# Two first products in full fp32, a shorter warm-up from a constant, and one load moved to another queue

## The chip, the core and the metric

The kernel runs on one core of a Trainium2 chip. The metric is device time in microseconds of one execution, lower is better; the time of a version is the median of its runs. A profile is one more execution, taken with the hardware profiler.

## What is computed

x is 2 x 512 x 512, so 1024 tokens of 512 features. Two blocks follow each other, each with a residual and a layer norm (all in fp32):

```python
# block 1
approx_up = x @ up_w.T ; gate_pre = x @ gate_w.T            # 512 -> 128 each
delta = gate_pre - local_point
approx_out = approx_up @ local_approx_output.T
for idx in range(6):                                         # Taylor-like terms of |delta|
    m = idx + 1
    dterm = exp(log|delta| * m - discount_factor[idx]) (* sign of delta if m is odd)
    tmp = dterm * approx_up (* (|delta| <= 2.5) if m > 4)
    approx_out += tmp @ fuse_weight[:, :, idx].T
ffn_out = silu(x @ ffn_gate_w.T) * (x @ ffn_up_w.T) @ ffn_down_w.T   # width 1248
x = layernorm(x + approx_out + ffn_out)
# block 2: weights first quantised to NF4 by blocks of 64 and dequantised, width 1376
x = layernorm(x + silu(x @ dq(w1).T) * (x @ dq(w2).T) @ dq(w3).T)
```

## The kernel before, in words

x is loaded transposed, with features on the partitions: four chunks `c` of 128 features by 1024 tokens, and each chunk has two halves `a` of 512 tokens (`HALF`). Below, x0a is chunk 0, first half, x0b its second half, x1a chunk 1, first half, and so on. They land in `xT_raw`, which is the start of the tile `h`; the profile calls them `h<-xT`.

TensorE's products are not plain fp32. Each operand is split into two fp32r numbers: ScalarE rounds it (`x_hi`, `w_hi`, in a helper at line 567), VectorE or GpSimd takes the remainder (`x_lo`, `w_lo`; lines 1032, 1037 and 1041 at the start), and TensorE adds up hi*hi, hi*lo and lo*hi, three matmuls of up to 512 columns. Everything but the two first stages below goes through the helper `product`, lines 1257 to 1259.

The first stage is the pair `up_w`, `gate_w`, together `w_pre`: for each of the four chunks, both `kind`s (0 and 1) and both halves, into the PSUM banks `2 * kind + half`. w_pre is loaded in three parts, 128 KB for chunk 0, 128 KB for chunk 1, 256 KB for the rest. TensorE takes chunk 0 by lines 1371 to 1382, six products for each half: for both kinds hi*hi (line 1376), w_lo*x_hi (1379), w_hi*x_lo (1382). Chunks 1 to 3 follow through `product`, and then the pairs of the gate and up weights (`w_in`), the output stage, and block 2. All of it is one fixed order on each engine, written out by hand, and engines wait for each other by counting semaphores.

Ahead of chunk 0 TensorE runs a warm-up: `WARM` fp32 products of 256 columns with zeros (line 1367) into an unused bank. The zeros are written by GpSimd into the tile `level` (line 1222), and TensorE waits for them.

The loads are issued by SyncE (`block.sync`) in this order: w_pre's first part, w_pre's second part (line 522), x1a, x1b (526), w_pre's rest (529), chunk 2 and chunk 3 (530), then w_in, the NF4 weights and so on (508, 511). ScalarE issues x0a and x0b (line 701) ahead of its first computation. The weights pass through five slots of the tile `raw` (`RAW_SLOTS`); load job `j` uses slot `j % 5`, and job 5 waits (`wait_split`) until job 0, which is w_pre, has been split.

Of the kernel before, what the change touches and what calls it, by code (L numbers as in the profile page):

```python
# [22 lines left out]
F32 = mybir.dt.float32  # L23
# [6 lines left out]
P = 128  # L30
TOK = 1024
D = 512
DC = D // P
HALF = 512
# [12 lines left out]
EPS = 1e-5  # L47
NR = 4
NL = 3
WARM = 5  # L50
BLOCK = 64
TINY = 1.1754943508222875e-38

# [71 lines left out]
def unit_width(u):  # L125
    if u < C2:
        return 2 * DC * min(P, F2 - u * P)
    return D * min(2, C2 - 2 * (u - C2))
# [55 lines left out]
RAW_SLOTS = 5  # L184
# [54 lines left out]
def rows(f, width):  # L239
    return min(P, width - f * P)  # L240


def job_rows(job):
    kind, f = job
    return P if kind == "fuse" else rows(f, F1) if kind == "out" else rows(f, F2)


def build(nc, xT, xN, w_pre, w_fuse, w_in, w_out, consts, w12, w3, w3_end, ident_in, out):
    with ExitStack() as ctx:  # L249
        def sb(name, shape, dt=F32):  # L250
            return ctx.enter_context(nc.sbuf_tensor(name, shape, dt))

        def sem(name):
            return ctx.enter_context(nc.semaphore(name))

        x_hi, x_lo = sb("x_hi", [P, DC, TOK], F32R), sb("x_lo", [P, DC, TOK], F32R)
# [6 lines left out]
        level = sb("level", [P, NL, UW])  # L263
# [8 lines left out]
        PS = ctx.enter_context(nc.psum_tensor("PS", [P, 8, 512], F32))  # L272

        xT_raw = h[:, 0:DC * TOK].rearrange("p (c t) -> p c t", c=DC)
# [21 lines left out]
        def w_raw(j):  # L296
            return raw[:, (j % RAW_SLOTS) * 1024:(j % RAW_SLOTS) * 1024 + 1024]

        def in_slot(w, i, n):
            return w[:, i % 2, 0:n]  # L300
# [14 lines left out]
        def job_shape(j):  # L315
            kind, f = JOBS[j]
            if kind == "pre":
                return P, 2 * DC * P
            if kind == "in":
                return P, 2 * DC * rows(f, F1)  # L320
            return job_rows(f), D
# [6 lines left out]

        s_line0 = sem("s_line0")
        s_ones = sem("s_ones")  # L330
        s_zero, s_warm = sem("s_zero"), sem("s_warm")
        s_pre_raw, s_pre_hi, s_pre_lo = [sem(f"s_pre_raw{c}") for c in range(2)], sem("s_pre_hi"), sem("s_pre_lo")
        s_point, s_ident = sem("s_point"), sem("s_ident")
        s_x = [sem(f"s_x{c}") for c in range(DC)]
        s_xb = [sem(f"s_x{c}b") for c in range(2)]
# [6 lines left out]
        s_xh, s_xl = sem("s_xh"), sem("s_xl")  # L342
        s_whi, s_wlo0, s_wlo = sem("s_whi"), sem("s_wlo0"), sem("s_wlo")
        s_wlo_in, s_wlo_v = sem("s_wlo_in"), sem("s_wlo_v")
        s_whi4, s_wlo4 = sem("s_whi4"), sem("s_wlo4")
        s_lhi, s_llo_t, s_llo_h = sem("s_lhi"), sem("s_llo_t"), sem("s_llo_h")
        s_pre, s_up, s_delta = sem("s_pre"), sem("s_up"), sem("s_delta")
        s_t, s_keep = sem("s_t"), sem("s_keep")
        s_pair, s_silu, s_h = sem("s_pair"), sem("s_silu"), sem("s_h")
# [21 lines left out]
        def wait_split(eng, j):  # L371

            if j < 2:
                eng.wait_ge(s_wlo0, j + 1)
            elif JOBS[j][0] == "in":
                eng.wait_ge(s_wlo_in, j - 1)
            elif j in VECTOR_LOW:
                eng.wait_ge(s_wlo_v, VECTOR_LOW.index(j) + 1)
            else:
                eng.wait_ge(s_wlo, j - C1 - sum(1 for x in VECTOR_LOW if x < j))  # L380
# [114 lines left out]
        @block.sync  # L495
        def _(sp):
            def load_job(j):
                kind, f = JOBS[j]
                if j >= RAW_SLOTS:
                    wait_split(sp, j - RAW_SLOTS)  # L500
                p, n = job_shape(j)
                if kind == "in":
                    src = w_in[:, f * 1024:f * 1024 + n]
                elif f[0] == "fuse":
                    src = w_fuse[f[1]]
                else:
                    src = w_out[f[1] * P:f[1] * P + p, :]
                sp.dma_start(w_raw(j)[0:p, 0:n], src).then_inc(s_raw[j % RAW_SLOTS], 16)

            def load_unit(u):  # L510
                sp.dma_start(unit_read(u), w12[:, u * UW:u * UW + unit_width(u)]).then_inc(s_q[u], 16)

            def load_residual(a):

                sp.wait_ge(s_llo_t, (G + 1) * (a + 1))
                sp.dma_start(R[:, TILES * a:TILES * (a + 1), :],
                             xN[:, TILES * a:TILES * (a + 1), :]).then_inc(s_R[a], 16)

            for c in range(DC):
                if c < 2:  # L520
                    part = slice(c * PRE0, (c + 1) * PRE0)
                    sp.dma_start(w_raw(0)[:, part], w_pre[:, part]).then_inc(s_pre_raw[c], 16)  # L522

                    for a in range(2 if c else 0):
                        ts = slice(a * HALF, (a + 1) * HALF)
                        sp.dma_start(xT_raw[:, c, ts], xT[:, c, ts]).then_inc((s_x, s_xb)[a][c], 16)
                    continue
                if c == 2:
                    sp.dma_start(w_raw(0)[:, 2 * PRE0:1024], w_pre[:, 2 * PRE0:1024]).then_inc(s_raw[0], 16)
                sp.dma_start(xT_raw[:, c, :], xT[:, c, :]).then_inc(s_x[c], 16)  # L530
            load_job(1)
            load_unit(0)
            sp.dma_start(term_consts[:], consts).then_inc(s_point, 16)
            load_unit(1)
            load_job(2)
            load_unit(2)
            for j in range(3, RAW_SLOTS):
                load_job(j)
            sp.dma_start(ident[:], ident_in).then_inc(s_ident, 16)
            for u in range(3, C2):  # L540
                load_unit(u)
            for j in range(RAW_SLOTS, len(JOBS)):
                if j == JOB[1, AGAIN[0]]:
                    load_residual(0)
                load_job(j)
            load_residual(1)
            for k in range(W3_UNITS):
                u = C2 + k
                if u < UNITS - 1:

                    wait_split(sp, max(j for j in range(len(JOBS)) if j % RAW_SLOTS == k))
                else:
                    sp.wait_ge(s_turn, 1)
                sp.dma_start(unit_read(u), (w3[:, k * UW:(k + 1) * UW] if u < UNITS - 1 else w3_end)).then_inc(s_w3[k], 16)

            for t in [t for t in range(TT) if t != TT - 2]:
                if t < TT - 1:
                    sp.wait_ge(s_norm, TT + t + 1)
                else:
                    sp.wait_ge(s_norm_last, 1)  # L560
                sp.dma_start(out[t * P:(t + 1) * P, :], R[:, t, :]).then_inc(s_out, 16)
            sp.wait_ge(s_out, 16 * TT)

        @block.scalar
        def _(act):
# [130 lines left out]
                copy(w_slot(2, ("w3", c), p)[0].rearrange("p (i b) -> p i b", i=SQ),  # L696
                     PS[0:p, w3_bank(c), :].rearrange("p (b i) -> p i b", i=SQ)).then_inc(s_whi4, 1)

            for a in range(2):
                ts = slice(a * HALF, (a + 1) * HALF)  # L700
                nc.scalar.dma_start(xT_raw[:, 0, ts], xT[:, 0, ts]).then_inc((s_x, s_xb)[a][0], 16)
            for c in range(DC):
                for a in range(2):
                    if c < 2 and a == 0:
# [6 lines left out]
                    ts = slice(a * HALF, (a + 1) * HALF)  # L711
# [60 lines left out]
            for n in range(PASS_START[2], len(SEQ)):  # L772
                if n + L_AHEAD < len(SEQ):
                    split_l(n + L_AHEAD)
                c = n - PASS_START[2]
# [390 lines left out]
        def _(pool):  # L1166
            g = nc.gpsimd
# [50 lines left out]
                pool.wait_ge(s_up2, k + 1)  # L1218
                g.tensor_tensor(dst, dst, up2[0:dst.shape[0], k % 2, :], ALU.mult).then_inc(s_h2, 1)  # L1219


            g.memset(level[:, 0, 0:P + 2 * P], 0.0).then_inc(s_zero, 1)
            for i in range(2 * C1):
                if i % 2 == 0 and i // 2 + 1 < C1:
                    lo_raw(JOB["in", i // 2 + 1])
# [27 lines left out]
        def _(pe):  # L1253
            t_ = nc.tensor
# [107 lines left out]
                last.then_inc(s_xtr, 1)  # L1362


            pe.wait_ge(s_zero, 1)
            for i in range(WARM):
                last = t_.matmul(PS[:, 7, 0:2 * P], level[:, 0, 0:P], level[:, 0, P:3 * P], start=True, stop=True)
            last.then_inc(s_warm, 1)
            wh0, wl0 = (in_slot(w, 0, 1024).rearrange("p (c g m) -> p g c m", g=2, c=DC) for w in (w_hi, w_lo))

            pe.wait_ge(s_pre_hi, 1)
            for half in range(2):
                xs = slice(half * HALF, (half + 1) * HALF)
                pe.wait_ge(s_xh, half + 1)
                for kind in (1, 0):
                    t_.matmul(PS[:, 2 * kind + half, :], wh0[:, kind, 0, :], x_hi[:, 0, xs], start=True, stop=False)
                pe.wait_ge(s_pre_lo, 1)
                for kind in (1, 0):
                    t_.matmul(PS[:, 2 * kind + half, :], wl0[:, kind, 0, :], x_hi[:, 0, xs], start=False, stop=False)
                pe.wait_ge(s_xl, half + 1)  # L1380
                for kind in (1, 0):
                    t_.matmul(PS[:, 2 * kind + half, :], wh0[:, kind, 0, :], x_lo[:, 0, xs], start=False, stop=False)
            for c in range(1, DC):
                if c == 1:
                    pe.wait_ge(s_pre_hi, 2)
# [4 lines left out]
                for kind, half in ((1, 0), (0, 0), (1, 1), (0, 1)) if c < DC - 1 else ((1, 0), (1, 1), (0, 0), (0, 1)):  # L1390
                    pe.wait_ge(s_xh, 2 * c + half + 1)
                    pe.wait_ge(s_xl, 2 * c + half + 1)
                    xs = slice(half * HALF, (half + 1) * HALF)
                    last = product(PS[:, 2 * kind + half, :], wh0[:, kind, c, :], wl0[:, kind, c, :],
                                   x_hi[:, c, xs], x_lo[:, c, xs], False, c == DC - 1)
# [21 lines left out]
            for n in range(PASS_START[2], PASS_START[3] - TAILS[2]):  # L1417
                c = n - PASS_START[2]
# [66 lines left out]
```

## Time and profile before

| | us |
|---|---|
| median of 3 runs | 411.65 (411.63 to 411.87) |
| the profiled execution | 412.71 |
| its span, first to last instruction | 410.8 |
| TensorE busy in it | 401.8 (98%) |
| VectorE, ScalarE, GpSimd busy | 325.1, 267.4, 290.1 |
| mean granted TensorE clock | 0.997 of full |

Times inside the profile count from the start of the span. `SPq` and `ACTq` are the issues of DMAs by SyncE and ScalarE, `PE` is TensorE's matmuls, `PEld` its weight loads. Matmul records overlap: one of 512 columns is drawn 0.39 us long while the next starts 0.23 us after it, so the distance between starts is what one costs.

### The profile page before, as it was taken

The page shows a single profiled execution, that of the slowest core. Times are in us where ns is not written, and L with a number is a line of the kernel's source. Part 1 is how long each engine was busy: PE and PEld are TensorE (multiplying, and loading weights), DVE is VectorE, ACT ScalarE, POOL GpSimd, SP SyncE. Part 2 cuts the span into 40 slices and gives each one's busy share as a digit, 9 for nine tenths or more (in the row PEclk, how much of TensorE's full clock was granted, in tenths as well). Part 3 has the DMA queues.
Part 4 walks back from the last instruction along what each step waited for, and adds up shares of the span by engine and source line. Part 5 has one row for each costly group of instructions (what it writes and reads, how often), then busy time and mean ns, then how long its engine had stood idle before and what let it go on. Part 6 is the DMA issues. An engine that isn't in the chain of part 4 may idle for free.

```text
span 410.8 us, 5355 instructions
## 1 busy us (share of the span) xinstructions
PE 401.8 (98%) x1770; PEld 327.9 (80%) x1770; DVE 325.1 (79%) x383; ACT 267.4 (65%) x372; POOL 290.1 (71%) x228
## 2 busy tenths in 40 slices
PE   7999999999999999999999999999999999999993
PEld 5888888888877888888888888888888877888872
DVE  3629989779888986999998799987779989935035
ACT  5575666677676847466956658888769777732613
POOL 0077998877978489936993366799999998954430
PEclk9999999999999999999999999999999999999998
DMA  7994101100204362103043000000000000000202
GB/s 258 409 408 146 53 14 51 28 26 0 53 3 123 89 224 69 27 0 104 1 131 146 0 2 1 2 0 0 2 2 0 2 0 0 2 0 2 102 0 102
DMA packets 10042, 26.48 MB, mean 64 GB/s; under 512 B 1248, under 2 KB 1632, under 8 KB 9760
## 3 DMA queue, kind: packets, MB, share of 16 engines
q1 hardware_dynamic: 9584, 25.37, 18.2%
q10 hardware_dynamic: 432, 0.79, 0.7%
q8 instruction: 14, 0.23, 0.2%
q14 instruction: 12, 0.10, 0.1%
HBM read 24.06 MB, written 2.10 MB: 64 GB/s over the span
## 4 chain that ended last, share of the span: by engine, by line
PE 95%; DMA 2%; DVE 1%; ACT 0%; issue 0%; POOLq 0%; SPq 0%; DVEq 0%; ACTq 0%
PE PS L1257 32%; PE PS L1258 31%; PE PS L1259 31%; DMA h<-xT 2%; PE PS L1361 1%; POOLq L249 0%; SPq L522 0%; ACT R L567 0%; DVE stats L933 0%; DVE R L928 0%; DVE x_lo L1041 0%; ACT x_hi L567 0%; ACT std L784 0%; DVE mv L959 0%; DVE std L972 0%
## 5 line engine op out<-in xcount | busy, mean ns | idle before, releaser
L1182 POOL TENSOR_SCALAR level<-side 128x1024 f32<-128x1024 int8 (+2 forms) x119 | 129.7, 1090 | 27.1 <-ACT side L567 13.0
L855 DVE TENSOR_TENSOR PS<-PS,level 128x1024 f32<-128x1024 f32 (+2 forms) x102 | 120.1, 1178 | 23.1 <-POOL level L1182 19.1
L1257 PE MATMUL PS<-x_hi,w_hi 128*128 128x512 f32 (+1 forms) x348 | 135.8, 390 | 0.9 <-DVE x_lo L1041 0.9
L1259 PE MATMUL PS<-x_hi,w_lo 128*128 128x512 f32 (+1 forms) x348 | 135.6, 390 | 0.0
L1258 PE MATMUL PS<-x_lo,w_hi 128*128 128x512 f32 (+1 forms) x348 | 135.5, 389 | 0.0
L567 ACT ACTIVATE side<-Q 128x1024 int8<-128x1024 f32 (+2 forms) x84 | 80.1, 997 | 17.2 <-DVE PS L851 15.2
L1257 PEld LDWEIGHTS PS<-x_hi,w_hi 128*128 128x128 f32 (+1 forms) x348 | 64.5, 185 | 16.1 <-issue 1.7
L1212 POOL TENSOR_TENSOR l_lo<-h,l_hi 128x512 fp32r<-128x512 f32 (+1 forms) x42 | 57.6, 1379 | 27.3 <-ACT l_hi L567 26.4
L1259 PEld LDWEIGHTS PS<-x_hi,w_lo 128*128 128x128 f32 (+1 forms) x348 | 64.5, 185 | 14.5
L1258 PEld LDWEIGHTS PS<-x_lo,w_hi 128*128 128x128 f32 (+1 forms) x348 | 64.5, 185 | 14.4
L1257 PE MATMUL PS<-x_hi,l_hi 128*128 128x512 f32 x144 | 56.1, 390 | 0.0
L1258 PE MATMUL PS<-x_lo,l_hi 128*128 128x512 f32 x144 | 56.1, 389 | 0.0
L1259 PE MATMUL PS<-x_hi,l_lo 128*128 128x512 f32 x144 | 56.0, 389 | 0.0
L650 ACT ACTIVATE h<-PS 128x512 f32<-128x512 f32 (+1 forms) x42 | 25.0, 594 | 34.3 <-PE PS L1259 34.0
L1201 POOL TENSOR_TENSOR w_lo<-raw,w_hi 128x1024 fp32r<-128x1024 f32 (+2 forms) x15 | 30.3, 2019 | 22.1 <-ACT w_hi L567 21.6
L1219 POOL TENSOR_TENSOR h<-h,Q 128x512 f32<-128x512 f32 (+1 forms) x22 | 30.3, 1376 | 18.2 <-ACT Q L567 15.9
L567 ACT ACTIVATE l_hi<-h 128x512 fp32r<-128x512 f32 (+1 forms) x42 | 25.9, 626 | 25.2 <-PE PS L1259 25.1
L567 ACT ACTIVATE side<-raw 128x1024 int8<-128x1024 f32 x35 | 35.1, 1058 | 6.1 <-DVE PS L851 6.1
L1257 PEld LDWEIGHTS PS<-x_hi,l_hi 128*128 128x128 f32 x144 | 27.0, 188 | 6.0 <-issue 0.4
L1257 PE MATMUL PS<-w_hi,l_hi 128*128 128x512 f32 (+1 forms) x80 | 31.5, 394 | 0.2 <-POOL l_lo L1212 0.2
L1259 PEld LDWEIGHTS PS<-x_hi,l_lo 128*128 128x128 f32 x144 | 27.0, 188 | 5.6
L1258 PEld LDWEIGHTS PS<-x_lo,l_hi 128*128 128x128 f32 x144 | 27.0, 188 | 5.6
(100 smaller groups left out, 510.6 us busy)
## 6 DMA issues: line engine op xcount, KB each, us to landing
Q<-w SPq DMA_DIRECT2D x10, 512.0 KB, 13.8
raw<-w_in SPq DMA_DIRECT2D x9, 512.0 KB, 12.3
raw<-w_out SPq DMA_DIRECT2D x14, 256.0 KB, 2.6
raw<-w SPq DMA_DIRECT2D x5, 512.0 KB, 3.8
R<-xN SPq DMA_DIRECT2D x2, 1024.0 KB, 5.4
raw<-w_fuse SPq DMA_DIRECT2D x7, 256.0 KB, 2.6
out<-R SPq DMA_DIRECT2D x7, 256.0 KB, 2.0
h<-xT SPq DMA_DIRECT2D x2, 512.0 KB, 8.1
```

The lines of the kernel that those rows point to most:

```text
L567: return nc.scalar.activation(dst, src, ACT.Copy, **kw)
L650: nc.scalar.activation(dst, PS[0:dst.shape[0], bank, :], ACT.Silu).then_inc(s_silu, 1)
L855: v.tensor_tensor(total, total, level_of(s), ALU.add).then_inc(s_add, 1)
L1182: g.tensor_scalar(level_of(s), side_of(s), LIMITS[k][1], LIMITS[k][0], ALU.min, ALU.max).then_inc(s_level, 1)
L1201: g.tensor_tensor(lo, w_raw(j)[0:p, 0:n], hi.bitcast(F32), ALU.subtract).then_inc(s_wlo_in if JOBS[j][0] == "in" else s_wlo, 1)
L1212: g.tensor_tensor(lo, view, hi.bitcast(F32), ALU.subtract).then_inc(s_llo_h, 1)
L1219: g.tensor_tensor(dst, dst, up2[0:dst.shape[0], k % 2, :], ALU.mult).then_inc(s_h2, 1)
L1257: t_.matmul(dst, a_hi, b_hi, start=start, stop=False)
L1258: t_.matmul(dst, a_hi, b_lo, start=False, stop=False)
L1259: return t_.matmul(dst, a_lo, b_hi, start=False, stop=stop)
L1361: last = t_.transpose(PS[:, XT_BANK + t % 2, c * P:(c + 1) * P], R[:, t, c * P:(c + 1) * P], ident[:])
```

## The change

TensorE's warm-up has four products in place of five and reads its zeros from the constant that the framework keeps (a 128 x 1 constant, repeated along the row), so that GpSimd's memset and the wait for it go. The first half of chunk 0 is computed by two fp32 products, one for each kind, straight from `raw` and `xT_raw`, in place of six split ones; the second half stays as it was, but waits for the counts that stood for half 1. x0a's load moves from ScalarE's queue to SyncE's, behind w_pre's first part; x0b stays on ScalarE's and is its only one. SyncE waits, ahead of job 5, which overwrites slot 0 of `raw`, until both fp32 products are done (`s_first`). ScalarE and VectorE still split x0a and w_pre, in the same order.

```diff
-WARM = 5
+WARM = 4
@@ load_job (SyncE)
                 if j >= RAW_SLOTS:
                     wait_split(sp, j - RAW_SLOTS)
+                if j == RAW_SLOTS:
+
+                    sp.wait_ge(s_first, 2)
@@ SyncE's first loads
                     sp.dma_start(w_raw(0)[:, part], w_pre[:, part]).then_inc(s_pre_raw[c], 16)
 
-                    for a in range(2 if c else 0):
+                    for a in range(2 if c else 1):
                         ts = slice(a * HALF, (a + 1) * HALF)
                         sp.dma_start(xT_raw[:, c, ts], xT[:, c, ts]).then_inc((s_x, s_xb)[a][c], 16)
@@ ScalarE
-            for a in range(2):
-                ts = slice(a * HALF, (a + 1) * HALF)
-                nc.scalar.dma_start(xT_raw[:, 0, ts], xT[:, 0, ts]).then_inc((s_x, s_xb)[a][0], 16)
+            nc.scalar.dma_start(xT_raw[:, 0, HALF:TOK], xT[:, 0, HALF:TOK]).then_inc(s_xb[0], 16)
@@ GpSimd
-            g.memset(level[:, 0, 0:P + 2 * P], 0.0).then_inc(s_zero, 1)
@@ TensorE
-            pe.wait_ge(s_zero, 1)
+            zeros = nc.const_aps.tensor(0.0, (P, 2 * P), F32)
             for i in range(WARM):
-                last = t_.matmul(PS[:, 7, 0:2 * P], level[:, 0, 0:P], level[:, 0, P:3 * P], start=True, stop=True)
+                last = t_.matmul(PS[:, 7, 0:2 * P], zeros[:, 0:P], zeros, start=True, stop=True)
             last.then_inc(s_warm, 1)
+            w_first = w_raw(0).rearrange("p (c g m) -> p g c m", g=2, c=DC)
+            pe.wait_ge(s_pre_raw[0], 16)
+            pe.wait_ge(s_x[0], 16)
+            for kind in (1, 0):
+                t_.matmul(PS[:, 2 * kind, :], w_first[:, kind, 0, :], xT_raw[:, 0, 0:HALF], start=True, stop=False).then_inc(s_first, 1)
             pe.wait_ge(s_pre_hi, 1)
-            for half in range(2):
-                xs = slice(half * HALF, (half + 1) * HALF)
-                pe.wait_ge(s_xh, half + 1)
...
+            pe.wait_ge(s_xh, 2)
+            for kind in (1, 0):
+                t_.matmul(PS[:, 2 * kind + 1, :], wh0[:, kind, 0, :], x_hi[:, 0, HALF:TOK], start=True, stop=False)
+            pe.wait_ge(s_pre_lo, 1)
+            for kind in (1, 0):
+                t_.matmul(PS[:, 2 * kind + 1, :], wl0[:, kind, 0, :], x_hi[:, 0, HALF:TOK], start=False, stop=False)
+            pe.wait_ge(s_xl, 2)
+            for kind in (1, 0):
+                t_.matmul(PS[:, 2 * kind + 1, :], wh0[:, kind, 0, :], x_lo[:, 0, HALF:TOK], start=False, stop=False)
```

## Rows read from the trace of the kernel before

**Rows 1.** The page: busy time by engine, and the chain that ended last by engine.

```profile
PE 401.8 (98%) x1770; PEld 327.9 (80%) x1770; DVE 325.1 (79%) x383; ACT 267.4 (65%) x372; POOL 290.1 (71%) x228
...
PE 95%; DMA 2%; DVE 1%; ACT 0%; issue 0%; POOLq 0%; SPq 0%; DVEq 0%; ACTq 0%
```

**Rows 2.** The chain that ended last, 0 to 12 us: start us, us, what.

```profile
1.64 6.56 DMA h<-xT
...
8.22 0.64 ACT x_hi L567
...
8.89 0.70 DVE x_lo L1041
...
9.72 0.47 PE PS L1257
```

**Rows 3.** The timeline of TensorE: start us, us, instruction, count, idle time before it.

```profile
5.83 0.70 PE L1376 MATMUL PS<-x_hi,w_hi 128*128 128x512 f32 x2
...
8.22 0.61 PE L1382 MATMUL PS<-x_lo,w_hi 128*128 128x512 f32 x2
...
11.85 0.39 PE L1257 MATMUL PS<-x_hi,w_hi 128*128 128x512 f32 x1
12.08 0.39 PE L1258 MATMUL PS<-x_lo,w_hi 128*128 128x512 f32 x1
12.31 0.39 PE L1259 MATMUL PS<-x_hi,w_lo 128*128 128x512 f32 x1
12.53 0.39 PE L1257 MATMUL PS<-x_hi,w_hi 128*128 128x512 f32 x1
```

**Rows 4.** The timeline, all engines: the start of the programs, and GpSimd's next work.

```profile
0.24 0.10 POOL L1478 MEMSET const-float32-0.0<- 128x1 f32 x1 [0.24 <-issue]
...
0.73 0.42 POOL L1222 MEMSET level<- 128x384 f32 x1 [0.29 <-POOLq L1478]
...
0.81 0.06 DVE L1022 MEMSET line<- 128x1 f32 x1 [0.81 <-PEq L1478]
...
1.20 4.56 PE L1367 MATMUL PS<-level 128*128 128x256 f32 x10 [1.20 <-POOL level L1222]
...
20.22 2.39 POOL L1201 TENSOR_TENSOR w_lo<-raw,w_hi 128x1024 fp32r<-128x1024 f32 x1 [19.07 <-ACT w_hi L567]
```

**Rows 5.** Timelines of warm-up records, cut so that their starts show; the transposes' chain row.

```profile
4.35 1.06 PE L1367 MATMUL PS<-level 128*128 128x256 f32 x2
...
4.78 0.99 PE L1367 MATMUL PS<-level 128*128 128x256 f32 x2
...
5.20 0.56 PE L1367 MATMUL PS<-level 128*128 128x256 f32 x1
...
195.41 0.87 PE PS L1361 x8
```

**Rows 6.** The timeline of ScalarE and VectorE: the splits of the first operands.

```profile
4.22 0.42 ACT L567 ACTIVATE w_hi<-raw 128x256 fp32r<-128x256 f32 x1 [1.28 <-DMA raw<-w_pre]
...
5.06 0.63 ACT L567 ACTIVATE x_hi<-h 128x512 fp32r<-128x512 f32 x1 [0.42 <-DMA h<-xT]
...
6.11 0.63 ACT L567 ACTIVATE x_hi<-h 128x512 fp32r<-128x512 f32 x1 [0.42 <-DMA h<-xT]
...
10.81 0.63 ACT L567 ACTIVATE x_hi<-h 128x512 fp32r<-128x512 f32 x1 [0.63 <-DMA h<-xT]
...
11.47 0.69 DVE L1041 TENSOR_TENSOR x_lo<-h,x_hi 128x512 fp32r<-128x512 f32 x1 [0.56 <-ACT x_hi L567]
```

**Rows 7.** The timeline of the DMA issues: SyncE's first ones and its first after a wait.

```profile
0.74 0.85 SPq L522 DMA_DIRECT2D raw<-w_pre  x2
1.64 0.90 SPq L526 DMA_DIRECT2D h<-xT  x2
...
3.06 1.01 SPq L530 DMA_DIRECT2D h<-xT  x2
...
18.02 2.32 SPq L508 DMA_DIRECT2D raw<-w_in  x2
```

**Rows 8.** Stretches of 1 us: busy by engine, clock, DMA share, GB/s.

```profile
2.00:3.00 1.00, 1.00 (x3) 0.80 (x3) 0.00 (x0) 0.94 (x1) 0.00 (x0) 1.00 0.92 281
3.00:4.00 1.00, 1.00 (x4) 0.75 (x3) 0.00 (x0) 0.00 (x0) 0.00 (x0) 1.00 1.00 203
...
7.00:8.00 1.00, 1.00 (x6) 0.79 (x6) 0.80 (x2) 0.05 (x1) 0.00 (x0) 1.00 1.05 391
```

More of the change, by code:

```diff
@@ L330, in build @@
         s_ones = sem("s_ones")
-        s_zero, s_warm = sem("s_zero"), sem("s_warm")
+        s_warm = sem("s_warm")
         s_pre_raw, s_pre_hi, s_pre_lo = [sem(f"s_pre_raw{c}") for c in range(2)], sem("s_pre_hi"), sem("s_pre_lo")
@@ L346, in build @@
         s_lhi, s_llo_t, s_llo_h = sem("s_lhi"), sem("s_llo_t"), sem("s_llo_h")
+        s_first = sem("s_first")
         s_pre, s_up, s_delta = sem("s_pre"), sem("s_up"), sem("s_delta")
@@ L1362, in transpose_x @@
                 last.then_inc(s_xtr, 1)
-            pe.wait_ge(s_zero, 1)
+            zeros = nc.const_aps.tensor(0.0, (P, 2 * P), F32)
             for i in range(WARM):
-                last = t_.matmul(PS[:, 7, 0:2 * P], level[:, 0, 0:P], level[:, 0, P:3 * P], start=True, stop=True)
+                last = t_.matmul(PS[:, 7, 0:2 * P], zeros[:, 0:P], zeros, start=True, stop=True)
             last.then_inc(s_warm, 1)
             wh0, wl0 = (in_slot(w, 0, 1024).rearrange("p (c g m) -> p g c m", g=2, c=DC) for w in (w_hi, w_lo))
-            pe.wait_ge(s_pre_hi, 1)
-            for half in range(2):
-                xs = slice(half * HALF, (half + 1) * HALF)
-                pe.wait_ge(s_xh, half + 1)
[L1375 to L1382, printed above, removed]
+            w_first = w_raw(0).rearrange("p (c g m) -> p g c m", g=2, c=DC)
[3 more added lines that the diff above has]
+                t_.matmul(PS[:, 2 * kind, :], w_first[:, kind, 0, :], xT_raw[:, 0, 0:HALF], start=True, stop=False).then_inc(s_first, 1)
+            pe.wait_ge(s_pre_hi, 1)
+            pe.wait_ge(s_xh, 2)
[7 more added lines that the diff above has]
+                t_.matmul(PS[:, 2 * kind + 1, :], wh0[:, kind, 0, :], x_lo[:, 0, HALF:TOK], start=False, stop=False)
             for c in range(1, DC):
```

## The prediction

> **What bounds the kernel now.** I read the page first, then the chain that ended last, then the first 13 us engine by engine, since every line of the change acts there. The page gives TensorE 401.8 of 410.8 us and the chain puts 95% on it, 2% on one transfer [rows 1]: the kernel is one long row of matmuls, and time can only be gained or lost where TensorE waits. The chain of the first 10 us shows the one early wait: the fourth DMA of the kernel (x's chunk 1, first half, "x1a" below) is issued at 1.64, lands 6.56 us later at 8.20, ScalarE rounds it (0.64), VectorE makes the remainder (0.70), and TensorE goes on at 9.72 [rows 2]. From there its products start 0.23 us apart up to 12.53, where chunk 2 begins [rows 3]. Before that wait TensorE had 12 products of chunk 0, the first at 5.83, the last pair from 8.22 [rows 3]; at 0.23 each they are issued out by 5.83 + 12 x 0.233 = 8.63. So it stands still for 9.72 - 8.63 = 1.1 us, and only for x1a. That is the fact on which all else hangs: whatever is done to chunk 0 before 9.72 is hidden as long as it is done by then, and nothing in it makes 9.72 earlier.
>
> **The warm-up.** It is five fp32 products of 256 columns, ten records, from 1.20 after a 0.42 us memset at 0.73 [rows 4]. The records start 0.427 us apart (4.35, 4.78, 5.20) [rows 5]. Each must be two passes of 256 columns, 512 column steps in 0.427 us, which is the 1.2 GHz level; from 5.83 a product of 512 columns takes 0.23 us, the 2.4 GHz level. The two passes are read from the transposes, whose records of 128 columns take 0.109 us, 256 steps at 2.4 GHz [rows 5]. So the granted clock rose between 5.2 and 6, after some 4.4 us of unbroken work; the clock column of the stretches says 1.00 from 2 us on already [rows 8], and there I go by the distance of the records. With the constant there is no memset to wait for. The constants are written by 0.24 and the other engines start their programs at 0.74 to 0.81 [rows 4], so I put TensorE's start at 0.8. One product less is 2 x 0.427 = 0.85 us less: the warm-up ends at 0.8 + 4.56 - 0.85 = 4.5 in place of 5.76. Cost and gain by themselves: nothing, as it lies before the wait. The memset off GpSimd is worth nothing either, since that engine next works at 20.22 [rows 4].
>
> **When the first product can start.** Now it needs w_pre's first part and x0a as loaded, and neither ScalarE's nor VectorE's pass. The first part of w_pre is ready at 4.22, x0a at 5.06, x0b at 6.11 [rows 6]. x0a came alone in ScalarE's queue with 512 KB moved in both queues; by the time of x0b, 768 KB were moved. With x0a second in SyncE's queue and x0b first in ScalarE's, x0a has up to 128 + 256 + 256 = 640 KB to share with. Halfway between 5.06 and 6.11 is 5.5, bounds these two. So the first product starts at about 5.6, 0.2 us before 5.83: what is saved on the roundings is mostly lost on the later x0a.
>
> **The fp32 pair.** Six split products (0.23 each, 1.40 us) go, two fp32 ones come. No fp32 product of 512 columns is in the trace. The nearest are the transposes, eight records (four fp32 products of 128 columns) in 0.87 us [rows 5], so 0.22 per 128 columns and 0.87 per 512 at the upper level; and the warm-up's 0.85 per 256 columns, so 1.71 per 512 at the lower level. I take 0.87, since the clock had risen by 5.8 in the trace, and keep 1.71 as the other end. The pair ends at 5.6 + 1.74 = 7.35: 0.34 us more work than it replaces. The second half's six products need ScalarE's x_hi of x0b: 5.5 + 2 x 0.63 = 6.8, and VectorE's x_lo by about 7.55, where TensorE asks for it at 7.35 + 4 x 0.23 = 8.3; no stall. They end at 7.35 + 1.40 = 8.75, against 8.63 before. TensorE then waits 0.95 us for x1a, if x1a comes as before. Net cost: nothing, with 0.95 us of cover.
>
> **The moved load.** One DMA goes over from ScalarE's queue to SyncE's and is issued ahead of w_pre's second part and all that follows; an issue takes 0.42 to 0.50 us there [rows 7]. So x1a, x1b, the rest of w_pre, chunks 2 and 3 and the first w_in are issued some 0.45 us later (x1a at 2.1). This is not on the path while the DMA engines are behind: they are 0.92 to 1.00 busy from 2 to 4 us [rows 8], x1a's issue at 1.64 stands 6.56 us from its landing, and in front of x1a lie the same bytes in either order (w_pre's two parts, x0a, x0b and itself, 1024 KB). So x1a should land at 8.2 again. What could shift it is how well the two queues move together: 203 GB/s between 3 and 4 us with both, 391 between 7 and 8 with SyncE's alone [rows 8]. With half as much in ScalarE's queue the mixed stretch is shorter, which speaks for a slightly earlier landing; the later issue speaks for a slightly later one. I allow x1a 0.35 us to either side and take zero. ScalarE itself is free 0.45 us earlier and waits for w_pre at 4.22 anyway. In the Trainium skill, "DMA: Bandwidth & Descriptors", section on queues, rings and completion order, each DMA engine is said to go round robin between the queues it has work for; by that x0b holds back x0a just as reckoned, and x1a's sum stays.
>
> **The rest.** SyncE's new wait for the two fp32 products stands before job 5, and all later weight loads are queued behind it. That load already waits until slot 0 is split and is issued no earlier than 18.02 [rows 7]; the products are over by 7.4, so it costs nothing (and would still with 9.0). Work after 9.72 is untouched.
>
> **The sum.** Against the profiled execution, 412.71 us with a span of 410.8: warm-up 0, first start 0, fp32 pair +0.34 covered by 0.95, moved load 0 +- 0.35; the sum is 412.7. The profiled execution lies 1.06 above the median of the runs, so the forecast is the median, 411.6.
>
> **Rivals.**
> (1) *The loads come earlier.* If x1a's lateness is due to the two queues mixing, TensorE goes on earlier. Alone this is soon used up: chunk 2's x_lo is ready at 11.47 + 0.69 = 12.16, about 0.13 more to hand over, where TensorE asks at 12.53 [rows 3, 6], so 0.24 us is all unless chunk 2 (ready 10.81) comes earlier as well. Both earlier by 0.35 to 1.0 gives 410.7 to 411.3. For it: the low rate from 3 to 4 us. Against: the same bytes in front, and no gap in the DMA engines' work.
> (2) *The clock rises too late* (the slower side). Between the warm-up's end at 4.5 and 5.6 TensorE now stands still for 1.1 us, before the rise that the trace has after 5.2. If the rise then needs a new unbroken stretch like the first (4.4 us), it comes at 5.6 + 4.4 = 10.0. The fp32 pair takes 3.4 us and ends at 9.0, then 2.3 products at 0.427 to 10.0 and 3.7 at 0.23, done at 10.8 where x1a's operands wait since 9.72: 1.1 us lost, 412.7. It decides from 0.95 us of lost time on. A rise at 9.0 loses 0.7 (9.0 + 6 x 0.23 = 10.4), one at 12 loses 2.1 (3.4 + 6 x 0.427 = 5.98, done at 11.6, and the next 0.4 us at half speed). So 412.3 to 413.8. For it: the gap is new, and it lies just where the clock was still low. Against: the wait of 0.9 us before 9.72 did not lower the clock in the trace, for the products behind it run 0.23 apart; and the work around the gap is 3.7 us before and 3.1 after. "TensorE: Matmul & The Clock Gate" of the Trainium skill, Part 1, says that "the default state is throttled, and activity releases the throttle", which speaks against a gap at this place and is this rival; by the rule alone the time would be the 412.3 to 413.8 above, and no row of the trace before shows a gap ahead of the rise.
> (3) *x1a comes over 0.35 us later*, through the later issue or because the two x0 halves fetched side by side disturb each other. It delays 9.72 one for one: 412.0 to 412.6.
> (4) *The change doesn't do what it says*: x0a lands as late as 6.1 and the pair starts after the splits would have been ready. The six products then end at 9.35, still before 9.72; no time lost. It is inside the forecast.
>
> **How the numbers follow.** The forecast with (4), 411.3 to 412.0: 0.62. Rival (1): 0.15, a third of it by more than 0.8 us. Rival (2): 0.15, most of it over 0.8 us. Rival (3): 0.08. A measurement of this kernel can tell 0.2%, 0.82 us, from no change: faster than 410.8 holds 0.06, slower than 412.5 holds 0.13, the rest 0.81. The range takes in the forecast, nearly all of (1) and (3) and the near half of (2): 410.9 to 412.9.
>
> **What would show it.** In the changed profile: the warm-up as eight records from about 0.8; the first fp32 record near 5.6 and four of them 0.43 apart (0.85 apart means the lower clock); the second half's six products over by 8.8; a wait for x_lo behind them of about 0.95 us; the product at 9.7. If that product is earlier by over 0.3, x1a's landing in the chain of waits will say so, and there must be a second look at chunk 2. If there is no wait ahead of it and its start is later, rival (2) is right. I am wrong, too, if an fp32 product costs more than the transposes say: at 1.71 each with the clock up, the second half would end at 10.4 and cost 0.7 us.

## The result and the profile after

| | before | after |
|---|---|---|
| median, 15 executions each | 411.70 (411.23 to 412.47) | 412.75 (411.78 to 414.17) |
| ratio | | 1.0028, 95% interval 1.0017 to 1.0039 |
| profiled execution, its span | 412.71, 410.8 | 412.39, 410.3 |

The change costs 1.05 us: the interval of the ratio lies above 1, and the loss is over the 0.82 us that the prediction took as the least that can be told from no change. The executions spread over 2.4 us in place of 1.2. The forecast was no change. A first puzzle stands in the last row: the two profiled executions come out the other way round. The one of before was 1.0 above its median, the one of after 0.4 below. The first views of the changed kernel are TensorE's timeline and the chain that ended last:

```profile
0.77 3.56 PE L1367 MATMUL PS<-const-float32-0.0 128*128 128x256 f32 x8 [0.77 <-PEq L1482]
5.50 1.95 PE L1376 MATMUL PS<-h,raw 128*128 128x512 f32 x4 [1.17 <-DMA h<-xT]
6.89 1.03 PE L1380 MATMUL PS<-x_hi,w_hi 128*128 128x512 f32 x2
...
8.21 0.61 PE L1386 MATMUL PS<-x_lo,w_hi 128*128 128x512 f32 x2
9.59 0.47 PE L1257 MATMUL PS<-x_hi,w_hi 128*128 128x512 f32 x1 [0.76 <-DVE x_lo L1043]
```

```profile
2.07 0.04 issue
2.11 5.95 DMA h<-xT
8.06 0.02 issue
8.08 0.64 ACT x_hi L571
8.73 0.02 issue
8.75 0.70 DVE x_lo L1043
9.45 0.14 issue
9.59 0.47 PE PS L1257
```

In this execution all came as forecast: eight records from 0.77, the pair at 5.50 (5.6 was said), the second half issued out by 8.7, a wait of 0.76 that the records show, and chunk 1 at 9.59, where [rows 2] have 9.72. The two profiles begin chunk 1 at nearly the same time, so the loss must be in executions that they do not show.

One number helps from here on. After chunk 1's first product nothing differs: in all 18 profiles below and the two first ones, the span less the start of that product lies between 400.6 and 401.2 (before 410.8 - 9.72 = 401.1, after 410.3 - 9.59 = 400.7). To half a microsecond, the span of an execution is decided by when chunk 1 begins; the 0.6 us between these numbers comes later in the kernel and does not go with the change (401.1 and 400.7 are both found in before).

The time of an execution holds a little more than its span, and that rest is not the same in all versions. It is 1.8 to 1.9 us in all executions of before whose span was kept, and 2.0 to 2.1 us in the versions below that have either the fp32 pair or one half of x's chunk 0 in SyncE's queue; in the changed kernel, which has both, it is 1.85 to 2.30, with a median of 2.08. So about 0.2 of the 1.05 us lies outside the span, where no row of a profile shows it. Its cause stays open; the median span of the changed kernel is 410.7, that of before 409.6 to 410.0 in the runs below.

### The profile page after: what moved, and what is told of

It reads as the page before. It is cut to its first block, busy times and chain, and to the rows that moved or that the text cites. A ratio compares the mean times of both kernels' runs of the same rounds, so it can differ in the third digit from the quotient of the medians.

```text
span 410.3 us, 5348 instructions
## 1 busy us (share of the span) xinstructions
PE 400.8 (98%) x1766; PEld 327.0 (80%) x1766; DVE 326.0 (79%) x383; ACT 267.4 (65%) x372; POOL 290.4 (71%) x227
## 4 chain that ended last, share of the span: by engine, by line
PE 96%; DMA 1%; DVE 1%; issue 0%; ACT 0%; POOLq 0%; SPq 0%; DVEq 0%; ACTq 0%
PE PS L1257 32%; PE PS L1258 32%; PE PS L1259 31%; DMA h<-xT 1%; PE PS L1361 1%; POOLq L249 0%; SPq L526 0%; ACT R L571 0%; DVE stats L935 0%; DVE R L930 0%; DVE x_lo L1043 0%; ACT x_hi L571 0%; SPq L530 0%; ACT std L786 0%; DVE mv L961 0%
```

## More profiles of both kernels

The expectations below weigh three theories. Theory 1: the standstill behind the shorter warm-up makes the clock rise late in a part of the executions. Theory 2: the fp32 pair's longer work. Theory 3: the moved load, which makes x's chunk 1 late. First the same code once more, for further profiles.

**before2**

> The kernel before once more, for a second profile. The first profiled execution took 412.71, the median is 411.65. If the wait for x's chunk 1 was peculiar to the slow execution: chunk 1's first half lands before 7.5 and TensorE goes through from 5.8 to chunk 1 without a wait, its first product at 8.6 to 8.7, time near 411.6. If the wait is always there: first product near 9.7.

**before3**

> The kernel before, for a third profile. x's chunk 1 landed at 8.20 (412.71) and 7.70 (411.88). If the median execution has no wait for it: landing at 7.5 or before, or products back to back from 5.8 to chunk 1, first product of chunk 1 at 8.6 to 9.0, time 411.3 to 411.8.

**after2**

> The changed kernel once more, for a second profile. The first was of an execution of 412.39, below its median of 412.75, and had the clock up before the first real product. If this one is slower than 412.7: theory 1 expects the fp32 records of 512 columns 0.85 us apart (0.43 in the first profile) and chunk 1's first product after 10.2 without a wait for x_lo; theory 3 expects them 0.43 apart, x's chunk 1 landing after 8.6 and a wait for x_lo of over 1 us.

**after3**

> The changed kernel once more, for a third profile, with the same two readings as the second. Chunk 1's first product comes at the time of the execution less 402.8 (first profile: 412.39 and 9.59).

| profile | time | ScalarE starts on x1a | chunk 1's first product |
|---|---|---|---|
| before | 412.71 | 8.22 | 9.72, after a wait |
| before2 | 411.88 | 7.72 | 9.34, no wait |
| before3 | 412.20 | 6.65 | 9.21, no wait |
| after | 412.39 | 8.08 | 9.59, after a wait |
| after2 | 412.84 | 7.81 | 10.34, no wait |
| after3 | 412.55 | 8.23 | 9.73, after a wait |

Chunk 0 in before2, TensorE's timeline (start us, us, instruction, count), where [rows 3] have products 0.23 apart from the first one on and a gap ahead of 9.72:

```profile
5.81 1.19 PE L1376 MATMUL PS<-x_hi,w_hi 128*128 128x512 f32 x2
6.80 0.85 PE L1379 MATMUL PS<-x_hi,w_lo 128*128 128x512 f32 x2
7.49 0.63 PE L1382 MATMUL PS<-x_lo,w_hi 128*128 128x512 f32 x2
...
8.88 0.62 PE L1382 MATMUL PS<-x_lo,w_hi 128*128 128x512 f32 x2
9.34 0.39 PE L1257 MATMUL PS<-x_hi,w_hi 128*128 128x512 f32 x1
```

The first pair to the second is 0.99 us, at 2.4 GHz it is 0.46 or a little over: the clock rose only at about 7.2, and there is no wait ahead of chunk 1. In before3 it rose at about 7.4 (its first three pairs start at 5.52, 6.51 and 7.37). Both come after a warm-up that runs up to the first product without a break, and neither execution is what was expected: x1a was there at 7.7 and by 6.65, but chunk 1 began at 9.34 and 9.21 and not at 8.6 to 9.0. So neither the wait nor a risen clock at 5.8 belongs to the kernel before; both vary from one execution to the next. With x1a early and the clock up, chunk 1 would begin at 5.83 + 12 x 0.23 = 8.6, a span of 409.2 to 409.8; of the 20 executions of before timed beside a_warm5, b_queue, c_warm4const and d_fp32, 11 have spans in this range, and 17 have at most 410.0. All three profiles of before are of executions slower than the median; the typical one is read from these spans and not from a profile.

after2 shows the slow side. Weight loads of TensorE, after2 first, then the first profile of after:

```profile
6.39 0.34 PEld L1376 LDWEIGHTS PS<-h,raw 128*128 128x128 f32 x1 [0.52 <-issue]
7.24 0.34 PEld L1376 LDWEIGHTS PS<-h,raw 128*128 128x128 f32 x1 [0.52 <-issue]
8.10 0.34 PEld L1380 LDWEIGHTS PS<-x_hi,w_hi 128*128 128x128 f32 x1 [0.52 <-issue]
```

```profile
6.00 0.19 PEld L1376 LDWEIGHTS PS<-h,raw 128*128 128x128 f32 x1 [0.24 <-issue]
6.43 0.19 PEld L1376 LDWEIGHTS PS<-h,raw 128*128 128x128 f32 x1 [0.24 <-issue]
6.86 0.19 PEld L1380 LDWEIGHTS PS<-x_hi,w_hi 128*128 128x128 f32 x1 [0.24 <-ACT w_hi L571]
```

0.85 against 0.43 apart: the pair's records run at the 1.2 GHz level, the pair takes 3.7 us of the chain and chunk 1 begins at 10.34, with no wait ahead:

```profile
5.40 3.71 PE PS L1376 x4
9.11 0.46 PE PS L1380 x2
9.57 0.46 PE PS L1383 x2
10.03 0.47 PE PS L1386 x2
```

That is rival (2), with its product at 10.3 where 10.4 was worked out for a rise at 9.0. In after and after3 the clock was up at about 5.4 despite the same gap, and there the late x1a decided. The rows of the warm-up seem to tell them apart already, after2 first, then after3:

```profile
0.77 3.75 PE L1367 MATMUL PS<-const-float32-0.0 128*128 128x256 f32 x8 [0.77 <-PEq L1482]
```

```profile
0.77 3.40 PE L1367 MATMUL PS<-const-float32-0.0 128*128 128x256 f32 x8 [0.77 <-PEq L1482]
```

The same eight records are drawn over 3.75 us in after2 and over 3.40 and 3.56 in after3 and after. The ends of matmuls are modelled, so this is a hint and no proof: where the clock had risen by the end of the warm-up, the gap took nothing back; where it had not, it stayed down until about 9. The two profiles of c_warm4const below part in the same way, 3.56 and 3.75.

## One part alone, or one part taken back

Versions that were timed together share a chip and its executions of before; a median is compared with before by the ratio.

**d_fp32: the pair alone**

```diff
 # kernel before, x0a and x0b on ScalarE's queue, WARM = 5 with the memset (shortened)
 # SyncE, ahead of job 5
+                if j == RAW_SLOTS:
+                    sp.wait_ge(s_first, 2)
 # TensorE
+            pe.wait_ge(s_pre_raw[0], 16)
+            pe.wait_ge(s_x[0], 16)
+            for kind in (1, 0):
+                t_.matmul(PS[:, 2 * kind, :], w_first[:, kind, 0, :], xT_raw[:, 0, 0:HALF], start=True, stop=False).then_inc(s_first, 1)
 # and the second half's six split products, as in the change
```

> The kernel before with the fp32 pair for the first half alone; warm-up of five with the memset, x's first two loads on ScalarE's queue. x's first half is there at 5.06, the warm-up ends at 5.76, the pair runs from 5.8 to 7.5, the second half's six products to 9.0: 0.7 us of cover left. Theory 1: no change, 411.4 to 412.0. Theory 2: 412.4 to 413. Theory 3: no change.

Measured: 412.02 (411.53 to 412.53), ratio 1.0012 (1.0003 to 1.0021), +0.38 us, between what theories 1 and 3 expected (at most 412.0) and what theory 2 did. Of this, 0.25 us is in the median span (410.0 against 409.75) and the rest outside it. The pair is 0.34 us longer than what it replaces, so most of this is paid: its cover, the wait, is mostly not there. Its chain (start us, us, what):

```profile
1.20 4.63 PE PS L1370 x10
5.83 1.99 PE PS L1378 x4
7.83 0.46 PE PS L1382 x2
```

The weight loads start 0.43 us apart from 6.38 on (6.80, 7.24), the upper level. The pair takes 1.99 us of this chain and not 1.74, as its first record, from 5.63, overlaps the end of the warm-up and still ran at the lower level for a part.

**c_warm4const: the shorter warm-up alone**

```diff
-WARM = 5
+WARM = 4
-            pe.wait_ge(s_zero, 1)
+            zeros = nc.const_aps.tensor(0.0, (P, 2 * P), F32)
 # the matmul reads zeros; GpSimd's memset is gone
```

> The kernel before with the shorter warm-up from the constant alone (four products, no memset); loads and split products as before. The warm-up ends at 4.3, the first real product at 5.8 needs the roundings: 1.5 us of standstill. Theory 1: a loss as in the changed kernel, median 412.2 to 413.0 with slow ones at 413.5 or more. In them the first twelve products stand 0.43 us apart. Theories 2 and 3: no change, 411.4 to 412.0.

**c_copy: the same, a second profile**

> The kernel before with four warm-up products from the constant, once more, for a second profile. The first was of an execution of 412.07, below its median of 412.69, with the clock up before the first real product at 5.82. Theory 1: in an execution of 412.6 or more the first real products stand 0.43 us apart and chunk 1's first product comes at 9.9 or later with no wait before it. Theory 3 has no reason for a loss here.

Measured: 412.69 (411.06 to 413.45), ratio 1.0026 (1.0013 to 1.0040); the second profile is of an execution of 413.22. Its TensorE:

```profile
0.77 3.75 PE L1366 MATMUL PS<-const-float32-0.0 128*128 128x256 f32 x8 [0.77 <-PEq L1477]
5.88 1.19 PE L1375 MATMUL PS<-x_hi,w_hi 128*128 128x512 f32 x2 [1.35 <-ACT x_hi L567]
6.87 1.05 PE L1378 MATMUL PS<-x_hi,w_lo 128*128 128x512 f32 x2
7.72 1.05 PE L1381 MATMUL PS<-x_lo,w_hi 128*128 128x512 f32 x2
8.57 1.05 PE L1375 MATMUL PS<-x_hi,w_hi 128*128 128x512 f32 x2
9.43 0.90 PE L1378 MATMUL PS<-x_hi,w_lo 128*128 128x512 f32 x2
...
10.62 0.40 PE L1256 MATMUL PS<-x_hi,w_hi 128*128 128x512 f32 x1
```

Pairs of products start 0.85 us and more apart up to 9.4, and chunk 1 starts at 10.62. In its first profile (412.07) the same pairs stood 0.54 and then 0.46 apart. So behind the shorter warm-up and a standstill of 1.35 to 1.5 us the clock rises late in a part of the executions, at about 10 in this one where before2 and before3 had 7.2 and 7.4, and the version costs a microsecond at the median with the old load order. Two profiles show that this happens and the median what it costs; they don't show how often. 411.06, in a kernel with that standstill, shows the other end.

**f_const6: no standstill**

```diff
 # c_warm4const, but
-WARM = 4
+WARM = 6
```

> The kernel before with the zeros from the constant and six warm-up products: warm-up from 0.77 to about 6.1, without a standstill before the first real product, which is 0.2 to 0.3 us later than before. Theory 1 (with four products the standstill makes the clock rise late): 411.6 to 412.1, narrow spread, well below the 412.69 of four products. Rival: reading the constant, or beginning earlier, is itself what costs; then it stays at 412.5 or more.

Measured: 411.22 (411.00 to 412.15), ratio 0.9994 (0.9985 to 1.0003). The warm-up runs from 0.77 to 6.2 and chunk 1 begins at 9.08. Two more products of zeros are worth 1.5 us at the median against c_warm4const (1.3 by the two ratios, as the chips differ), more than was expected (411.6 to 412.1); neither the constant nor the early start costs anything.

**b_queue: the moved load alone**

```diff
-                    for a in range(2 if c else 0):
+                    for a in range(2 if c else 1):
 # and ScalarE issues x0b only, as in the change
```

> The kernel before with the move of x's first load to SyncE's queue alone, warm-up of five with the memset, split products. Theory 1: no change against before (411.4 to 412.0), since the warm-up runs on until 5.76 and the first product comes at about 6.0. Theory 2: no change. Theory 3: 412.4 to 413 with a wide spread.

Measured: 412.99 (412.15 to 413.41), ratio 1.0036 (1.0022 to 1.0049). The interval reaches down into that of c_warm4const, so it isn't shown to be the dearer of the two; but it is over 1 us where I had put zero.

**b_copy and b_copy2: the same, for profiles**

> The version with the moved load alone, for a second profile. Its median is 412.99, that with the halves exchanged 411.61, though the DMAs are the same in number, size and order. Reading A (the first product starts later and, with a standstill behind the warm-up that ends at 5.83, the clock rises late): first twelve products partly 0.43 us apart, chunk 1's first product at 10 or later without a wait. Reading B (x's chunk 1 lands late): products 0.23 apart, chunk 1 landing at 8.4 or later with a wait of over 1 us.

> The same once more, for a third profile, with the same two readings.

413.33 and 412.62. Timeline rows of b_copy, TensorE and ScalarE:

```profile
8.49 0.61 PE L1380 MATMUL PS<-x_lo,w_hi 128*128 128x512 f32 x2
10.59 0.47 PE L1255 MATMUL PS<-x_hi,w_hi 128*128 128x512 f32 x1 [1.49 <-DVE x_lo L1039]
...
9.09 1.24 ACT L567 ACTIVATE x_hi<-h 128x512 fp32r<-128x512 f32 x2 [2.31 <-DMA h<-xT]
```

Reading B: chunk 0 was over at 8.9, and ScalarE sat 2.3 us until x1a was there at 9.07. In b_copy2 x1a was there at 8.33 and the wait was short (0.30), since the clock had also been late: there both readings hold.

**b_const6: the moved load with an unbroken warm-up**

```diff
 # b_queue with the zeros from the constant and
-WARM = 5
+WARM = 6
```

> The version with the moved load, with the zeros from the constant and six warm-up products, which run without a break from 0.77 to about 6.1, when x0a's rounding is done too. The same without the moved load took 411.22. Reading A (clock): 411.3 to 411.8. Reading B (chunk 1 lands late): 412.4 to 413.

Measured: 412.71 (412.07 to 413.40), ratio 1.0021 (1.0011 to 1.0030). The same without the move was 0.9994. So the clock is not what the move costs: 0.27% of 411.7, some 1.1 us, stay with a warm-up of six products (in its profile a gap of 0.39 us is left ahead of the first real one, at 6.04, and the products behind it stand 0.23 apart).

**a_warm5 and k_noqueue5: the changed kernel mended in one place and in two**

```diff
 # a_warm5: the change with
-WARM = 4
+WARM = 5
 # k_noqueue5: a_warm5, and x0a back on ScalarE's queue
-                    for a in range(2 if c else 1):
+                    for a in range(2 if c else 0):
...
-            nc.scalar.dma_start(xT_raw[:, 0, HALF:TOK], xT[:, 0, HALF:TOK]).then_inc(s_xb[0], 16)
+            for a in range(2):
+                ts = slice(a * HALF, (a + 1) * HALF)
+                nc.scalar.dma_start(xT_raw[:, 0, ts], xT[:, 0, ts]).then_inc((s_x, s_xb)[a][0], 16)
```

> The changed kernel with five warm-up products in place of four: the warm-up ends at about 5.2 us in place of 4.3 (its last record then starts near 4.75), so TensorE stands still for about 0.2 us in place of 1.1 us ahead of the first real product at 5.5. Theory 1 (the standstill ahead of the rise of the granted clock makes the rise late in a part of the executions): the loss goes; median 411.5 to 411.8, the slowest execution under 412.6, and spread as narrow as that of the kernel before. Theory 2 (the loss is the fp32 pair's longer work, or its slower rate): stays near 412.7. Theory 3 (the moved load makes x's chunk 1 late in a part of the executions): stays near 412.7 with slow ones near 414.

> The changed kernel with five warm-up products and with x's first two loads both back on ScalarE's queue; the constant and the fp32 pair stay. The five runs so far say that each part costs by itself, so the wait for x's chunk 1 that the profile of before shows is absent in most executions. Theory 3, now: most of the loss of the version with five warm-up products (412.70) is the moved load; then this one is at 411.4 to 411.9 (pair from about 5.3 to 7.1, second half to 8.5, against 8.6 before). Theory 1, the late clock alone: it stands still from about 5.3 to the same first product as with the moved load, so 412.5 to 413.

Measured: a_warm5 412.70 (411.96 to 413.76), ratio 1.0026 (1.0013 to 1.0038): nothing regained at the median, so theory 1 alone is not the answer. k_noqueue5 411.60 (411.23 to 412.33), ratio 1.0000 (0.9991 to 1.0009): all of it, as theory 3 expected. That a chunk 1 that comes late covers a late clock would explain the first; it was not shown by itself. With the load back, five warm-up products from the constant pay for the longer pair, which begins at 5.17.

The difference of the medians to before on the same chip, and how much of it is in the span:

| version | time | of it in the span (medians) | n |
|---|---|---|---|
| d_fp32 | +0.38 | +0.25 | 11 |
| c_warm4const | +1.05 | +1.15 | 7 |
| f_const6 | -0.40 | -0.4 | 11 |
| b_queue | +1.35 | +1.25 | 5 |
| b_const6 | +0.88 | +0.7 | 11 |
| a_warm5 | +1.06 | +0.8 | 8 |
| k_noqueue5 | -0.02 | -0.2 | 11 |

The constant and the length of the warm-up leave the rest outside the span as it is; the pair or the moved load adds about 0.2 us to it, both together 0.2 to 0.3.

## What is it about the moved load?

**g_issue: the later issue alone**

```diff
                     sp.dma_start(w_raw(0)[:, part], w_pre[:, part]).then_inc(s_pre_raw[c], 16)
+                    if c == 0:
+                        sp.dma_start(term_consts[:], consts).then_inc(s_point, 16)
...
-            sp.dma_start(term_consts[:], consts).then_inc(s_point, 16)
```

> The kernel before with the 3.5 KB load of the constants term_consts moved to the second place of SyncE's queue, so that w_pre's second part and x's chunk 1 are issued about 0.45 us later, with nearly no bytes ahead of them and x's chunk 0 untouched. If the moved load costs by the later issue of what is behind it: 412.4 to 413, as with the moved load alone (412.99). If it costs by x's first half landing later, or by the way that the two queues share the DMA engines: 411.4 to 411.9.

Measured: 411.15 (410.62 to 412.08), ratio 0.9990 (0.9980 to 0.9999). x1a is issued at 2.11, as in b_queue, but lands at 6.4. The later issue is not the cause. x0a came at 4.4 (5.06 in [rows 6]).

**p_swap: the same DMAs with the halves exchanged**

```diff
-                    for a in range(2 if c else 1):
+                    for a in range(0 if c else 1, 2):
-            nc.scalar.dma_start(xT_raw[:, 0, HALF:TOK], xT[:, 0, HALF:TOK]).then_inc(s_xb[0], 16)
+            nc.scalar.dma_start(xT_raw[:, 0, 0:HALF], xT[:, 0, 0:HALF]).then_inc(s_x[0], 16)
```

> The version with the moved load alone, but with the halves exchanged: x0b second in SyncE's queue, x0a alone in ScalarE's. Number, size and order of the issues are the same, so x's chunk 1 should land as with the moved load alone; x0a lands as early as before or earlier. If the moved load costs by x0a's lateness: 411.2 to 411.9. If it costs by chunk 1 landing later: 412.6 to 413.2 as with the moved load alone (412.99).

**p_copy: the same, a second profile**

> The moved load with the halves exchanged, for a second profile. In the first, x's chunk 1 landed at 6.73; with the halves as in the change it landed at 8.35, 9.07, 8.33 and 7.92 in the four profiles of versions with the move and split products. If which half goes through which queue decides where chunk 1 lands: again before 7.7 here. If 6.73 was chance: 8.0 or later, and the median of 411.61 has another reason.

Measured: 411.61 (410.90 to 412.22), ratio 0.9996 (0.9987 to 1.0005); p_copy 410.89. By the expectation this time would have spoken for x0a's lateness; but the profiles show x1a early too, and that was taken as the same in both. The stretches from 5 to 6 us (length, busy share and count of PE, PEld, DVE, ACT and POOL, clock, DMA share, GB/s), in this order p_swap, p_copy, b_queue, b_copy, after2 and after3:

```profile
5.00:6.00 1.00, 1.00 (x3) 0.73 (x3) 0.98 (x3) 1.00 (x3) 0.00 (x0) 1.00 1.09 372
```

```profile
5.00:6.00 1.00, 1.00 (x5) 0.69 (x5) 0.88 (x3) 0.92 (x3) 0.00 (x0) 1.00 1.05 405
```

```profile
5.00:6.00 1.00, 0.84 (x2) 0.14 (x2) 0.44 (x2) 0.77 (x2) 0.00 (x0) 1.00 0.80 255
```

```profile
5.00:6.00 1.00, 0.25 (x2) 0.00 (x0) 0.22 (x2) 0.68 (x2) 0.00 (x0) 1.00 0.69 230
```

```profile
5.00:6.00 1.00, 0.60 (x1) 0.50 (x2) 0.07 (x2) 0.71 (x2) 0.00 (x0) 1.00 0.90 267
```

```profile
5.00:6.00 1.00, 0.66 (x2) 0.45 (x3) 0.11 (x1) 0.77 (x2) 0.00 (x0) 1.00 0.95 255
```

ScalarE's wait for x1a in p_swap, in p_copy and in after3 (the first and last of which, with after2, ran on the same chip):

```profile
6.75 0.63 ACT L567 ACTIVATE x_hi<-h 128x512 fp32r<-128x512 f32 x1 [0.60 <-DMA h<-xT]
```

```profile
6.32 1.32 ACT L567 ACTIVATE x_hi<-h 128x512 fp32r<-128x512 f32 x2
```

```profile
8.23 1.25 ACT L571 ACTIVATE x_hi<-h 128x512 fp32r<-128x512 f32 x2 [1.55 <-DMA h<-xT]
```

In the eight profiles with x0a in SyncE's queue ScalarE starts on x1a at 7.54 to 9.09, half of them after 8.2; with x0b there at 6.75 and 6.32; with both in ScalarE's queue and the small load second in SyncE's, at 6.42 and 6.92 (g_issue, gc5); with the order of before, at 6.65 to 8.22 in eight profiles. The ranges of the first and the last group overlap; their middles are 8.2 and 7.7. The load in ScalarE's queue lands at about 4.5 and the one in SyncE's at about 5.2 with either order of the halves; what differs is the stretch behind it. Number, size and place of the issues are the same in b_queue and p_swap, so none of them is the cause. Why the halves matter was not settled; that it has to do with the addresses is a guess.

The exchange also brings x0a's rounding forward, from 5.23 in b_queue to 4.61 in p_swap, and TensorE's first real product from 6.00 to 5.36, so the two medians alone don't tell whether x0a or x1a costs the time. The rows do, for the versions with split products: b_queue, b_copy, b_copy2 and b_const6 all have a wait for x1a's operands ahead of chunk 1 (0.87, 1.49, 0.30 and 0.40 us), so there x1a sets the start, and an earlier x0a alone would have moved nothing.

**gc5: what helped, together**

```diff
 # g_issue, with the zeros from the constant and no memset; WARM stays 5
```

> The kernel before with both changes that came out at or under it: the small load second in SyncE's queue (411.15) and the zeros from the constant, five warm-up products, so that the warm-up runs from 0.77 to 5.2, where x0a's rounding is done at about 5.1. No fp32 pair, no moved load. If the two gains add: 410.8 to 411.2. If the earlier end of the warm-up leaves a standstill where x0a lands as usual: 411.4 or more.

Measured: 411.12 (410.54 to 411.90), ratio 0.9989 (0.9980 to 0.9999), against 0.9990 for g_issue alone: the two don't add, but this version and g_issue are under the kernel before by a little more than the interval. In its profile chunk 1 begins at 8.43.

## Why the prediction was wrong, step by step

- **What bounds the kernel: wrong, and the step that failed.** "Whatever is done to chunk 0 before 9.72 is hidden as long as it is done by then": I took the 1.1 us wait ahead of 9.72 [rows 2, 3] as a property of the kernel and hid everything in it. It was one execution, 1.06 us above the median; the text even says so in its sum, and doesn't ask why. The span less 401 gives chunk 1 at 9.7 for it, and at 8.5 to 9.1 for the median (411.65 less the 1.9 that lie around the span, less 401.2 to 400.6), and 12 products from 5.83 end at 8.6. The wait is absent in before2 and before3. So in place of 0.95 us of cover there is between none and 0.5 at the median, and d_fp32 says nearly none: of its 0.34 us of longer work, 0.25 is in the span (its whole cost is 0.38 us, with an interval of 0.1 to 0.9). With the cover gone, every part of the change is priced anew.
- **The warm-up: the time right (0.77, ten records less two), its price wrong.** "Cost and gain by themselves: nothing" leaves out that the clock may not have risen by the first real product, and that the gap can put this off to 9 or 10. (Two small misreadings: the zeros' constant is written from 0.24 on and not by then [rows 4], and the warm-up ended at about 4.3 and not 4.5; nothing hangs on them.) Alone it costs 1.05 us (c_warm4const), with six products nothing (f_const6).
- **The first product at 5.6: right**, 5.50, 5.40 and 5.34.
- **The fp32 pair: right in size.** 0.43 for each record at 2.4 GHz, 0.85 at 1.2 GHz, as worked out from the transposes and the warm-up [rows 5]; 0.34 us longer. "Net cost: nothing" failed with the cover: 0.38 us (d_fp32).
- **The moved load, 0 +- 0.35: the second term that failed.** Same bytes ahead, so same landing, does not hold: alone it costs 1.35 us, and taking it back regains 1.1 (a_warm5 to k_noqueue5). Rival (3), a later x1a at 412.0 to 412.6, had this right and was given 0.08, but both of its causes are refuted: the later issue by g_issue, the two halves of x0 fetched side by side by p_swap, which fetches them so too. The cause stays open. The round-robin rule of the Trainium skill ("DMA: Bandwidth & Descriptors", the section on queues, rings and completion order) agrees with x0a's landing at 5.0 to 5.4 beside x0b, where x0a alone in ScalarE's queue lands at about 4.5, but p_swap, equal by that rule, lands x1a over a microsecond earlier than b_queue.
- **Rival (2), the late clock: right as mechanism**, in one of three profiles of the changed kernel, at 412.84 with chunk 1 at 10.34, and the likely source of executions up to 414.17 (a span of 412.2, so chunk 1 at about 11.5, where a rise at 12 was worked out to give 11.6); for these there is no profile, and this is not shown. It was given 0.15. As "TensorE: Matmul & The Clock Gate" of the Trainium skill says (Part 1), activity releases the throttle. A gap before that costs in some executions (after2, c_copy) and in others not (after, after3); and the clock was late in before2 and before3 without a gap, which the rival left out: it took the rise at 5.2 to 6 of one execution as fixed.
- **The rest: right.** Behind chunk 1 all spans agree to 0.6 us, so SyncE's new wait costs nothing that shows. What lies outside the span was not thought of: 0.2 us.
- **The sum.** Parts alone are +0.38, +1.05 and +1.35, together +1.05 and not 2.8: a late clock and a late x1a meet at one point, chunk 1, and only the later one counts. It is this overlap, and not the cover, that kept the median inside the stated range.

## What to carry to other kernels

Before a wait in one profile is used as cover, compare that execution with the median: where it is slower by as much as the wait is long, the wait may be what made it slow, and the typical execution may pay for an edit in full. Take two or three profiles of the same code, and compare the spans as well as the times. Let a warm-up last until the first real product is ready: here, running it a little too long cost nothing (f_const6) and a gap of 1.4 us cost a microsecond (c_warm4const). When loads are reordered at the start, measure the landing of the ones behind, since equal bytes and equal issues did not give equal landings.

## What I had not expected of the hardware

- The clock's rise moves from one execution to the next with the same code: in before it was up at 5.8, or only at about 7.2 and 7.4 (before2, before3), in each case behind work without a break from 1.20 on. Of the ten profiles with the memset and five warm-up products, four have it past 7; with four warm-up products it was up at the first real product, 5.5, or down until about 9 (after, after2) and about 10 (c_copy).
- Exchanging two 256 KB halves between two queues moved a third load's landing from 7.9 to 9.1 (four profiles) down to 6.7 and at most 6.3 (two), and the rate from 5 to 6 us from 230 to 281 up to 372 and 405 GB/s.
- With a 3.5 KB load put second in SyncE's queue, x0a landed at 4.4 in both profiles (4.7 to 5.1 in the eight with the order of before), and the kernel was 0.1% faster, at the edge of its interval.
- The time outside the span was 1.8 to 1.9 us in some versions and 2.0 to 2.1 in others, though the edits between them touch only the first 10 us.
